# Second block's softmax: the shift and the sums on VectorE, one exponential per eight heads

## The reference

```python
scores = jnp.einsum('bhqd,bhkd->bhqk', q, k) / math.sqrt(D_K)
p_attn = jax.nn.softmax(scores, axis=-1)
x = jnp.einsum('bhqk,bhkd->bhqd', p_attn, v)
```

## Time and profile before

| what | us |
|---|---|
| median of 3 runs (lowest, highest) | 1882.35 (1881.37, 1883.09) |
| the profiled execution | 1880.03 |
| its span, first to last instruction | 1878.3 |

### The profile page before, as it was taken

How to read it: one execution, slowest core, us unless ns; L and a number is a source line. 1 busy time by engine, 2 the same in 40 slices (tenths; PEclk the granted TensorE clock), 3 DMA queues, 4 the chain that set the end, 5 groups by cost and what they waited for, 6 DMA issues and landing times. The chain is left out here.

```text
span 1878.3 us, 33112 instructions
## 1 busy us (share of the span) xinstructions
PE 1338.2 (71%) x9000; PEld 1136.6 (61%) x9001; DVE 1257.1 (67%) x3313; ACT 831.8 (44%) x2767; POOL 1008.0 (54%) x1247
## 2 busy tenths in 40 slices
PE   6604559600037676676865899998589999999997
PEld 4403446400025455565654677776479999999997
DVE  4499999999988999999775143454344444444442
ACT  5521224501113666666866487886323323322332
POOL 3258998886669999899866334342111121122121
PEclk9857778955568788888976999998689999999999
DMA  4611113630031011010112111133130410411200
GB/s 118 209 38 32 43 40 118 214 77 0 27 114 38 23 33 34 20 30 19 28 33 84 50 49 44 53 120 111 33 118 20 142 59 20 146 55 44 76 17 7
DMA packets 107864, 119.21 MB, mean 63 GB/s; under 512 B 22225, under 2 KB 87176, under 8 KB 105736
## 3 DMA queue, kind: packets, MB, share of 16 engines
q1 hardware_dynamic: 70216, 90.98, 15.6%
q10 hardware_dynamic: 33136, 18.58, 3.4%
q0 software_dynamic: 4432, 8.73, 1.4%
HBM read 83.44 MB, written 35.74 MB: 63 GB/s over the span
## 5 line engine op out<-in xcount | busy, mean ns | idle before, releaser
L242 POOL TENSOR_TENSOR wt<-wt 128x1024 f32<-128x1024 f32 x128 | 301.3, 2354 | 47.2 <-DVE wt L187 32.2
L248 POOL TENSOR_TENSOR wt<-wt 128x512 f32<-128x512 f32 (+2 forms) x384 | 306.7, 799 | 30.1
L1887 PE MATMUL e_ph<-e_g,e_w 128*128 128x128 f32 x2496 | 285.2, 275 | 0.7 <-ACT e_g L1857 0.7
L1887 PEld LDWEIGHTS e_ph<-e_g,e_w 128*128 128x128 f32 x2496 | 281.9, 192 | 0.9 <-issue 0.9
L187 DVE SCALAR_TENSOR_TENSOR wt<-wt,scan 128x256 f32<-128x256 f32 x512 | 241.7, 472 | 1.8 <-POOL wt L242 1.7
L166 DVE TENSOR_REDUCE wt<-wt 128x16 f32<-128x272 f32 x512 | 218.9, 428 | 0.1
L177 DVE TENSOR_TENSOR scan<-wt,scan 128x256 f32<-128x256 f32 x512 | 214.8, 419 | 0.3
L155 DVE TENSOR_TENSOR wt<-wt,scan 128x256 f32<-128x256 f32 x512 | 209.8, 410 | 0.5 <-PEq L265 0.5
L1370 ACT ACTIVATE wt<-p_pX,p_mx 128x120 f32<-128x120 f32 x512 | 176.4, 386 | 75.2 <-DVE p_mx L1156 73.4
L1502 PE MATMUL p_pm<-p_w_mix,p_oT 128*128 128x256 f32 x128 | 43.8, 502 | 198.9 <-DMA p_oT<-o 169.0
L1766 POOL TENSOR_TENSOR e_ve<-e_mv,eps 128x1 f32<-128x1 f32 x39 | 7.4, 190 | 330.6 <-DVE e_mv L1822 330.6
(11 more groups left out here) (221 smaller groups left out, 2807.4 us busy)
## 6 DMA issues: line engine op xcount, KB each, us to landing
wt<-in_L_ffn_W SPq DMA_DIRECT2D x24, 1024.0 KB
qkv<-f_st ACTq DMA_DIRECT2D x48, 256.0 KB, 2.3
p_kE<-kE SPq DMA_DIRECT2D x16, 480.0 KB, 3.7
p_vP<-vP SPq DMA_DIRECT2D x16, 480.0 KB
wt<-qkv SPq DMA_DIRECT2D x6, 1024.0 KB, 10.1
e_xt<-routed ACTq DMA_DIRECT2D x39, 130.0 KB, 2.1
f_xt<-in_x SPq DMA_DIRECT2D x16, 256.0 KB, 2.8
p_oT<-o SPq DMA_DIRECT2D x16, 256.0 KB, 2.8
```

The costliest lines, as they stand in the source:

```text
L242: nc.gpsimd.tensor_tensor(x, s["S"][:, h, z * Q:(z + 1) * Q], s["qn"][:, h, z * Q:(z + 1) * Q].rearrange("p t (o d) -> p t o d", o=1).to_b ...
L248: nc.gpsimd.tensor_tensor(x[:, :, :, 0:half], x[:, :, :, 0:half], x[:, :, :, half:2 * half], ALU.add).then_inc(s["o_fold"][h], 1)
L1887: ins = nc.tensor.matmul(ph2[:, c // 2, c % 2], w2[:, s, i, c * P:(c + 1) * P], g1[:, i], start=(i == 0), stop=(i == C1 - 1))
```

## The change

For the second block alone, VectorE adds the negated maximum to a group's 8 x 120 scores and writes the result to `pr` (`shifted`, right behind each `maximum`). ScalarE then takes one exponential over the 960 elements, in place in `pr`, without bias and without sums. VectorE makes the sums of a sequence's 16 heads by one reduction over 1920 elements ahead of the reciprocal (`sums_of`). The first block is as it was.

```diff
+            def shifted(c, x):
+                dve.wait_ge(max_done, c * HALVES + (x + 1))
+                dve.wait_ge(PT_done, c * 8)
+                heads = slice(x % 2 * HG, (x % 2 + 1) * HG)
+                nc.vector.tensor_tensor(pr[:, x // 2, heads].rearrange("p (r x) c -> p r x c", r=2), scores(x),
+                                        mx[:, x // 2, heads].rearrange("p (r x o) -> p r x o", r=2, o=1).to_broadcast([P, 2, HG // 2, CTX]),
+                                        ALU.add).then_inc(shifted_done, 1)
+
+            def sums_of(n, q):
+                dve.wait_ge(exp_done, n * HALVES + 2 * (q + 1))
+                dve.wait_ge(rec_done, n * 2)
+                nc.vector.tensor_reduce(sm[:, q], pr[:, q], AX, ALU.add).then_inc(summed, 1)
+
-            def inverse_sums(n, q):
-                dve.wait_ge(exp_done, n * HALVES + 2 * (q + 1))
+            def inverse_sums(jb, n, q):
+                if late(jb, n):
+                    sums_of(n, q)
+                    dve.wait_ge(summed, n * 2 + (q + 1) - 2 * M)
+                else:
+                    dve.wait_ge(exp_done, n * HALVES + 2 * (q + 1))
...
                     maximum(c, 0)
+                    if late(jb, c):
+                        shifted(c, 0)
...
-            def exponential(c, x):
+            def exponential(jb, c, x):
+                if late(jb, c):
+                    act.wait_ge(shifted_done, c * HALVES + (x + 1) - HALVES * M)
+                    p = pr[:, x // 2, x % 2 * HG:(x % 2 + 1) * HG]
+                    nc.scalar.activation(p, p, ACT.Exp).then_inc(exp_done, 1)
+                    return
```

More of the change, by code:

```diff
@@ L879, in scan_and_post @@
                                     "rec_done", "norm_done"))
+        shifted_done, summed = sem("p_shifted_done"), sem("p_summed")
         (PT_done, PT_out, pv_done, pv_out, att_done, r2_done, mv2_done, rs2_done, x2_done, x2T_done,
@@ L1251, in step @@
                     maximum(c, 1)
+                    if late(jb, c):
+                        shifted(c, 1)
                 scan(5)
@@ L1255, in step @@
                     maximum(c, 2)
+                    if late(jb, c):
+                        shifted(c, 2)
                 scan(7)
                 if "c" in on:
-                    inverse_sums(c, 0)
+                    inverse_sums(jb, c, 0)
                     if late(jb, c):
@@ L1270, in step @@
                     maximum(c, 3)
+                    if late(jb, c):
+                        shifted(c, 3)
                 scan(10)
@@ L1281, in step @@
                 if "c" in on:
-                    inverse_sums(c, 1)
+                    inverse_sums(jb, c, 1)
                 scan(14)
@@ L1441, in step @@
                 if "c" in on:
-                    exponential(c, 0)
-                    exponential(c, 1)
+                    exponential(jb, c, 0)
+                    exponential(jb, c, 1)
                 if "d" in on:
@@ L1446, in step @@
                 if "c" in on:
-                    exponential(c, 2)
+                    exponential(jb, c, 2)
                 if "b" in on:
@@ L1455, in step @@
                         normalise(c, 0)
-                    exponential(c, 3)
+                    exponential(jb, c, 3)
                 if "a" in on:
```

## The result

The changed kernel takes 1904.34 us (median of 4 runs, 1900.17 to 1908.89), beside 1882.72 us for the kernel before (4 runs, 1881.37 to 1883.85). The ratio is 1.0116, with a 95% interval of 1.0086 to 1.0145, so it is slower by 16 to 27 us. The forecast was 1907 us.

The account below looks back on a forecast made before the run. TensorE was taken to set the pace in the filled steps, with a margin of 0.2 us. Order and durations (18.1 us) plus clock (6.8) made 24.9 us on 1882.35: 1907 us, range 1894 to 1921.

Parts of the forecast that it names:

- The prices: Added instructions in the second block: VectorE's addition 1.15 us and sums 2.15 us, ScalarE's single exponential 1.0 us.
- The walk to `attended`: Filled steps 15 to 18: VectorE's `attended` ends 2.6 us later, so TensorE idles 2.5 us ahead of stage a.
- The other waits: TensorE waits 3 to 3.5 us for exponential 3 in steps 14 and 19, near 9.7 for `x2` in step 20.
- Order and durations alone: Steps 14 to 21: 18.1 us more, 8.9 in the filled steps and 9.2 in the other four.
- The clock: TensorE's clock falls behind six new idle stretches (steps 14 to 19), four in six, 1.7 us each: 6.8 us.
- GpSimd shut out: Sums or additions on VectorE block GpSimd's work for `second_norm`, so `x2` comes later: 14 us more, 1921; chance 0.12.
- The clock holds: No clock fall behind the new gaps: 18.1 us more, 1900; chance 0.2 within the forecast's case.
- no change: TensorE does not see the later `attended`: 1882 us; chance 0.05.
- faster: VectorE's added work up to `attended` fits in 0.69 us of waits, leaving ScalarE's shorter exponentials: about 4 us, 1878; chance 0.03.

Follow-up runs that it names:

- product_late: The changed kernel with only the product of sequence 0 moved behind stage d's statistics, its sums staying ahead of `attended`: 1886.58 us, 1.0033 of the kernel before.
- sums_late: The changed kernel with the sums, reciprocal and product of sequence 0 moved behind stage d's statistics: 1874.92 us, 0.9967 of the kernel before.
- filled_short: The changed kernel plus unread matmuls in TensorE's gaps, five ahead of stage a (steps 15 to 18), six ahead of `gate_up` 2 (14, 19): 1896.95 us.
- shift_only: The kernel before plus VectorE's addition of the maximum; ScalarE keeps eight exponentials a group, from SBUF, with their sums: 1891.09 us, ratio 1.0059.

## Why the prediction was right

The forecast held, by the steps it named.

- **The prices.** The addition took 1.16 us (1.15 forecast), the sums 2.14 and 2.15 (2.15), the exponential 1.00 (1.0).
- **The walk to `attended`.** 2.6 us later, and a wait ahead of stage a of 2.37 to 2.46 us, where 2.5 was forecast. product_late, where it is 0.39 us and those for the exponential of group 3 are 0.82 and 0.74 us, shows what these waits cost: the clock stays at 1.00 from step 14 to 19, and the stretch is 17.5 us shorter, the new wait for `x2` counted in. sums_late, which also puts the sums of sequence 0 behind the hand-over, has the same instructions and is 28 us shorter.
- **The other waits.** For the exponential of group 3, 3.07 and 2.98 us in steps 14 and 19 (forecast 3 to 3.5); for `x2` none in the filled steps, and 9.41 us in step 20 (9.7).
- **Order and durations alone: mis-sized.** The term was 18.1 us; filled_short shows 14.0. The filled steps get 1.9 us longer and not 2.2, step 14 1.8 and not 2.1, step 19 1.85 and not 2.25, step 20 2.5 and not 3.4, and step 21 0.2 and not 1.4. The last two are half of the error, and not all of that is the walk's. From the first maximum to the transposes of `x2`, step 20 got 3.1 us longer (18.95 to 22.05 us) and step 21 0.9 us (17.26 to 18.20). What follows the transposes took 0.6 and 0.7 us less than before; in step 20 that is the clock (0.74 and not 0.71: the eight projection matmuls took 1.94 us and not 2.54), in step 21 it is not taken apart.
- **The clock: mis-sized the other way.** The term was 6.8 us, from four falls in six gaps at 1.7 us each. There were five falls, in both samples, and they cost 9.6 us in the profiled execution (about 5 by the medians). The price was taken from one fall to 0.72. But of the four falls that the forecast had counted, one was to 0.50 for the whole 6 us (from 754.67 us, behind 2.74 us), and it left out a seventh gap of that size that began at full clock, in step 21 (2.23 us idle, then 0.58 from 1319.63 us). In the changed kernel two of the five falls lasted the whole window (0.50).
- **Luck.** The two errors nearly cancel: 14.0 + 9.6 = 23.6 us against 24.9. The mechanism was right, but a forecast within 3 us of the median is better than its terms were.
- **GpSimd shut out (0.12): refuted for this change.** The sums of sequence 1 in the changed kernel ran from 1172.33 for 2.15 us, and GpSimd's four small operations ran beside them undisturbed:

```profile
1172.40 0.19 POOL L1064 TENSOR_TENSOR p_ve<-p_mv,eps 128x2 f32<-128x2 f32 x1 [2.42 <-DVE p_mv L1143]
1172.67 0.71 POOL L1068 TENSOR_TENSOR p_rs<-p_ve,exponent 128x2 f32<-128x2 f32 x1
1173.46 0.19 POOL L1070 TENSOR_TENSOR p_scaled_mean<-p_mv,p_rs 128x2 f32<-128x2 f32 x1
1173.73 0.20 POOL L1072 TENSOR_TENSOR p_shift<-empty,p_scaled_mean 128x2 f32<-128x2 f32 x1
```

  By the rule of the Trainium skill ("SBUF — State Buffer", section "SBUF: two separate sides") a VectorE operation with two SBUF inputs and a GpSimd operation that reads SBUF exclude each other for a whole instruction, and one with a single SBUF input does so only in a two-port mode. The traces agree in both halves: 0.71 us beside the sums, 2.57 and 2.62 us beside a product.
- **The clock holds, no change, faster.** None of them came. What the last one named, ScalarE's shorter exponentials, is worth something only once VectorE's work is out of the way of `attended`: that is sums_late. Compared with before, its step 14 has no wait for the exponential of group 3, step 19 one of 0.48 us (1.14), and the 0.31 us for `x2` in the filled steps are gone.

What stays open. The gap of 2.37 us in step 15 was not followed by a lower clock, the three of 2.45 and 2.46 us were, in both samples, and so was one of 1.86 us in shift_only; the length of the gap alone does not tell them apart, and nothing here says what does. The clock's price is known only as 5 to 10 us. And the 4.9 us before step 14 were not explained beyond that such differences appear between kernels whose code is the same there.

## What to carry to other kernels

An engine at 43% of a stretch is not free: what counts is what stands in its list ahead of the instruction that the busy engine waits for. Before work is moved to it, walk that list to the next hand-over, and put the new work behind the hand-over; here that turned 22 us lost into 6 us won with the same instructions. An order is good or bad only with what stands in it: the same move made the kernel before 13 us slower, since it put two products beside GpSimd's small operations, where the changed kernel has the sums between them.

## What the runs showed of the hardware

- The product over two SBUF operands and GpSimd delay each other in both directions: GpSimd's 0.7 us operation took 2.57 us behind a product, and the product took 3.05 and 3.14 us in place of 2.16 while GpSimd ran its 512-element addition.
- At full clock, TensorE idle for 2.45 us was followed by 6 us at a granted clock of 0.50, and matmuls of 1.97 us took 3.75 (steps 16 and 18). Gaps of 1.86 us (shift_only) and of 2.46, 2.98 and 3.07 us were followed by 0.72 to 0.74, one of 2.37 us by 1.00. Filling the gaps with matmuls that nothing reads kept the clock at 1.00 and took 9.6 us off the stretch.
- Step 14, up to which the instructions are the same in all eleven profiled executions, began up to 11 us apart from one to another.
